# A fused attention and mixture-of-experts kernel: the order of the last two heads, of the last batch's routing, and of the first expert's rows

## The reference

```python
# first block: attention with squared scores and a decay
qk = einsum('bthd,bshd->bhts', q, k) * scale
a = where(causal, qk**2 * exp(logG[t] - logG[s]), 0)
y = einsum('bhts,bshd->bthd', a, v) / (sum(a, -1) + 1e-6)
x1 = layernorm(x + y.reshape(B, T, 2048) @ Wc + bc)
# second block: 6 of 64 experts for each token, and a shared one
scores = softmax(x1 @ gate_w.T); w, idx = top_k(scores, 6); w /= sum(w)
# rows of x1 go to (expert, place in it); places beyond the capacity are dropped
eo = (silu(buf @ w_gate[e].T) * (buf @ w_up[e].T)) @ w_down[e].T
y = sum of w * eo over a token's experts + (silu(x1 @ sg.T) * (x1 @ su.T)) @ sd.T
out = layernorm(x1 + y)
```

## Time and profile before

| | |
|---|---|
| median of 3 runs | 2256.55 us (2251.35 to 2260.19) |
| profiled execution | 2263.97 us |
| its span | 2262.2 us, mean granted clock of PE 0.979 |
| busy: PE, PEld | 2145.9 us (95%), 1960.7 us (87%) |
| busy: DVE, ACT, POOL | 1293.0 (57%), 1162.2 (51%), 751.1 us (33%) |

### The profile page before, as it was taken

The page is one execution under the profiler, slowest core; times in us unless marked ns, Lnnn a source line. Parts: engine busy times, 40 slices in busy tenths (PEclk is TensorE's granted clock), DMA queues, the critical chain, the costliest instruction groups (busy, mean ns, idle before and its releaser), DMA issues.

```text
span 2262.2 us, 38643 instructions
## 1 busy us (share of the span) xinstructions
PE 2145.9 (95%) x14567; PEld 1960.7 (87%) x14570; DVE 1293.0 (57%) x2851; ACT 1162.2 (51%) x2201; POOL 751.1 (33%) x751
## 2 busy tenths in 40 slices
PE   8999999999999999999999999999886899999993
PEld 6999998999889899889989898999765789999992
DVE  4444444444666345455644556545663688888876
ACT  4444544444444445444444444445433577777875
POOL 3121112100004520000352001440242478878885
PEclk9999999999999999999999999999997999999996
DMA  4866732112112311211241211321343789999977
GB/s 168 334 275 263 294 107 71 46 61 73 36 59 97 134 53 54 80 36 56 82 140 58 80 61 51 102 83 63 107 150 133 184 198 237 235 221 238 234 154 239
DMA packets 146642, 302.28 MB, mean 134 GB/s; under 512 B 20336, under 2 KB 82544, under 8 KB 146448
## 3 DMA queue, kind: packets, MB, share of 16 engines
q1 hardware_dynamic: 104960, 247.34, 32.2%
q0 software_dynamic: 41056, 51.96, 11.6%
q10 hardware_dynamic: 432, 0.44, 0.1%
HBM read 160.57 MB, written 142.67 MB: 134 GB/s over the span
## 4 chain that ended last, share of the span: by engine, by line
PE 79%; DVE 8%; issue 4%; ACT 3%; POOL 3%; DMA 2%; another core or an unknown queue 1%; POOLq 0%; ACTq 0%; SPq 0%; DVEq 0%
PE bank L951 48%; PE bank L1360 21%; PE bank L960 5%; PE bank L1373 2%; POOL y_part L2421 2%; PE bank L1478 1%; DMA y_part<-y_e,row_token 1%; DVE ub L1966 1%; DVE xe_lo L2243 1%; DVE stats L2326 0%; DVE bank L2150 0%; ACT q_hi L1638 0%; ACT silu_b L1712 0%; POOL slots L2411 0%
## 5 line engine op out<-in xcount | busy, mean ns | idle before, releaser
L1360 PEld LDWEIGHTS bank<-v,a 128*128 128x128 f32 x4608 | 605.5, 191 | 44.2 <-ACT a L1662 0.5
L1360 PE MATMUL bank<-v,a 128*128 128x129 f32 x4608 | 618.6, 275 | 0.3 <-ACT a L1662 0.3
L2421 POOL DMA_INDIRECT y_part<-y_e,row_token x234 | 359.1, 1535 | 147.9 <-ACT y_e L1779 77.1
L2394 POOL TENSOR_TENSOR decay_all<-decay_all,tab 128x128 f32<-128x128 f32 x128 | 60.2, 471 | 918.3 <-DMA decay_all<-decay_dram 917.9
L1658 ACT ACTIVATE a<-bank,c_s 128x512 f32<-128x512 f32 x384 | 263.1, 686 | 184.2 <-PE bank L951 170.8
L1662 ACT ACTIVATE a<-ub 128x512 f32<-128x512 f32 (+1 forms) x256 | 133.8, 523 | 376.9 <-DVE ub L1966 355.3
L2411 POOL DMA_INDIRECT slots<-rows,slot_u x192 | 189.2, 985 | 319.6 <-PE bank L1360 140.8
L951 PE MATMUL bank<-q_hi,k_hi 128*128 128x512 f32 (+1 forms) x640 | 262.9, 411 | 7.5 <-DVE ub L1966 7.5
L1945 DVE TENSOR_TENSOR q_lo<-bank,q_hi 128x512 fp32r<-128x512 f32 x128 | 88.5, 692 | 273.2 <-ACT q_hi L1638 269.8
L951 PE MATMUL bank<-q_lo,k_hi 128*128 128x512 f32 (+1 forms) x640 | 238.5, 373 | 0.0
L951 PE MATMUL bank<-q_hi,k_lo 128*128 128x512 f32 (+1 forms) x640 | 237.3, 371 | 0.0
(11 more groups left out here) (247 smaller groups left out, 4761.8 us busy)
## 6 DMA issues: line engine op xcount, KB each, us to landing
slots<-acc SPq DMA_DIRECT2D x64, 816.0 KB, 7.8
w_raw_f<-in_wffn SPq DMA_DIRECT2D x68, 624.0 KB
decay_all<-decay_dram SPq DMA_DIRECT2D x128, 128.0 KB
xr<-slots SPq DMA_DIRECT2D x18, 544.0 KB
xr<-slots SPq DMA_DIRECT2D x20, 476.0 KB
w_hi<-w_dram SPq DMA_DIRECT2D x24, 384.0 KB
w_lo<-w_dram SPq DMA_DIRECT2D x24, 384.0 KB
wc_hi<-wc_dram SPq DMA_DIRECT2D x24, 256.0 KB
```

The source lines that it names most:

```text
L1360: ins = e.matmul(dst[:, tt, r, :], a32[u % NA][:, r, t0:t0 + P], v[n % 3][:, s, :], start=(s == 0 and r == 0), stop=(s == 2 * g + tt), ski ...
L2394: e.tensor_tensor(arg[:, GROUP:GROUP + P], arg[:, P:GROUP], mask, ALU.add)
L2421: e.indirect_dma_start(out=y_part[part], out_offset=bass.IndirectOffsetOnAxis(ap=token, axis=0), in_=y_rows, in_offset=None, bounds_check= ...
```

## The change

The last two heads take turns by groups of queries: group 2 of each, then group 3 of each, with the places of `em`, `decay_all` and the loads of the decay taken by the group's number in the order (`em_at`). The last batch is routed in three parts, a half and two quarters. The steps of the first half, and those of the first quarter up to `softmax0`, are tied to units by a table, `route_at`; `TOGETHER` is gone. Both sends of the first half are now in the attention. A part of one pair has no `again`. The shared jobs are no longer split around the routing in the same places, and the first expert's rows are turned ahead of the last `shared_end`. The buffers of the experts' rows are taken by `x_at(place)`; with M1 = 6 blocks this is the parity of the place, as before. Two of ACT's copies of shared results no longer wait for the store of x1t.

```diff
-LAST_UNITS = (diagonal(LAST, 0) + before(LAST, 1) + before(LAST + 1, 1)[:1] + diagonal(LAST, 1) + before(LAST + 1, 1)[1:]
-              + diagonal(LAST + 1, 0) + diagonal(LAST + 1, 1) + before(LAST, 2) + before(LAST, 3) + diagonal(LAST, 2)
-              + diagonal(LAST, 3) + before(LAST + 1, 2) + before(LAST + 1, 3) + diagonal(LAST + 1, 2) + diagonal(LAST + 1, 3))
+HEAD_A, HEAD_B = LAST, LAST + 1
+LAST_UNITS = (diagonal(HEAD_A, 0) + before(HEAD_A, 1) + before(HEAD_B, 1)[:1] + diagonal(HEAD_A, 1) + before(HEAD_B, 1)[1:]
+              + diagonal(HEAD_B, 0) + diagonal(HEAD_B, 1) + before(HEAD_A, 2) + before(HEAD_B, 2)[:2] + diagonal(HEAD_A, 2)
+              + before(HEAD_B, 2)[2:] + before(HEAD_A, 3)[:2] + diagonal(HEAD_B, 2) + before(HEAD_A, 3)[2:] + before(HEAD_B, 3)
+              + diagonal(HEAD_A, 3) + diagonal(HEAD_B, 3))
...
-PARTS = [(b_, 0, TILES) for b_ in range(B - 1)] + [(B - 1, t_, TILES // 2) for t_ in (0, TILES // 2)]
+PARTS = ([(b_, 0, TILES) for b_ in range(B - 1)] + [(B - 1, 0, TILES // 2)]
+         + [(B - 1, t_, TILES // 4) for t_ in (TILES // 2, TILES * 3 // 4)])
+FIRST_HALF, QUARTER_A, QUARTER_B = B - 1, B, B + 1
...
-             + [f"{what}{q}" for q in pairs for what in ("again", "send")])
+             + [f"{what}{q}" for q in pairs for what in ("again", "send") if what == "send" or len(pairs) > 1])
...
-TOGETHER = ("stat0", "norm0", "norm1", "store", "softmax1", "chosen_bf", "weight0")
...
-        "em": {(L, 0): -5, (L, 1): -3, (L + 1, 0): 0, (L + 1, 1): 4, (L, 2): 12, (L, 3): 17, (L + 1, 2): 26, (L + 1, 3): 31},
-        "em_mask": {(L, 0): -7, (L, 1): -4, (L + 1, 0): -1, (L + 1, 1): 1, (L, 2): 10, (L, 3): 15, (L + 1, 2): 24, (L + 1, 3): 29},
-        "decay_in": {(L, 0): -11, (L, 1): -7, (L + 1, 0): -4, (L + 1, 1): -2, (L, 2): 1, (L, 3): 5, (L + 1, 2): 13, (L + 1, 3): 18}}
+        "em": {(L, 0): -5, (L, 1): -3, (L + 1, 0): 0, (L + 1, 1): 4, (L, 2): 12, (L + 1, 2): 17, (L, 3): 26, (L + 1, 3): 31},
+        "em_mask": {(L, 0): -7, (L, 1): -4, (L + 1, 0): -1, (L + 1, 1): 1, (L, 2): 10, (L + 1, 2): 15, (L, 3): 24, (L + 1, 3): 29},
+        "decay_in": {(L, 0): -11, (L, 1): -7, (L + 1, 0): -4, (L + 1, 1): -2, (L, 2): 1, (L + 1, 2): 5, (L, 3): 13, (L + 1, 3): 18}}
     cols_at = {-3: (1, 0, 0), -2: (0, 0, 0), -1: (0, 1, 0), 4: (1, 0, 1), 7: (0, 0, 1), 10: (0, 1, 1)}
-    first_half_routed_at = 19
+    route_at = {17: [(FIRST_HALF, "stat0")], 18: [(FIRST_HALF, "stat1"), (FIRST_HALF, "std")],
+                20: [(FIRST_HALF, step) for step in ("norm0", "norm1", "store")], 22: [(FIRST_HALF, "x1t0")],
+                23: [(FIRST_HALF, "logit0")], 24: [(FIRST_HALF, "x1t1")], 25: [(FIRST_HALF, "logit1")],
+                26: [(FIRST_HALF, "softmax0")], 27: [(FIRST_HALF, "softmax1"), (FIRST_HALF, "max")], 28: [(FIRST_HALF, "index")],
+                29: [(FIRST_HALF, "hot0"), (FIRST_HALF, "chosen0")],
+                30: [(FIRST_HALF, step) for step in ("hot1", "chosen1", "chosen_bf")],
+                31: [(FIRST_HALF, step) for step in ("weight0", "weight1", "count")] + [(QUARTER_A, "stat0")],
+                32: [(FIRST_HALF, "slots"), (QUARTER_A, "std")], 33: [(FIRST_HALF, "again0"), (FIRST_HALF, "send0")],
+                34: [(FIRST_HALF, "again1"), (FIRST_HALF, "send1")], 35: [(QUARTER_A, "norm0"), (QUARTER_A, "store")],
+                37: [(QUARTER_A, "x1t0")], 38: [(QUARTER_A, "logit0")], 39: [(QUARTER_A, "softmax0")]}
...
-        elif background and u >= step_from and background[0] != (B - 1, "again1"):
+        elif background and u >= step_from:
             p, name = background.pop(0)
             route_step(p, name)
-            while p == B - 1 and name in TOGETHER:
-                p, name = background.pop(0)
-                route_step(p, name)
-
             step_from = u + (2 if p < B - 2 else 1)
...
+    def turn(x_id):
+        for pair in range(pairs_of(x_id)):
+            on_spare("turn_x", x_id, pair)
+        do("pick", x_id)
+
+    def split(x_id):
+        do("split_hi", x_id)
+        for part in range(3):
+            do("split_lo", x_id, part)
+
     catch_up()
     do("shared_in", 2)
     up(0, 0)
     do("experts_begin")
     send_all()
+    on_spare("project", L, NG - 1)
+    on_spare("turn", L + 1, NG - 1)
     up(0, 1)
-    on_spare("turn", HEADS - 1, NG - 1)
-    do("turn_lo", HEADS - 1, NG - 1)
+    do("add", L, NG - 1)
+    do("turn_lo", L + 1, NG - 1)
+    route(QUARTER_A, "softmax1", "max", "index")
+    on_spare("project", L + 1, NG - 1)
     up(0, 2)
     gated(0, 0)
-    on_spare("project", HEADS - 1, NG - 2)
+    do("add", L + 1, NG - 1)
+    route(QUARTER_B, "stat0", "std")
     gated(0, 1)
-    up(1, 0)
-    do("add", HEADS - 1, NG - 2)
-    on_spare("project", HEADS - 1, NG - 1)
-    route_to("stat0")
+    route(QUARTER_A, "hot0", "chosen0", "chosen_bf")
+    up(1)
+    route(QUARTER_A, "weight0", "weight1", "count")
     gated(0, 2, 3)
-    up(1, 1)
-    do("add", HEADS - 1, NG - 1)
     do("shared_in", 3)
-    route_to("std")
-    up(1, 2)
+    route(QUARTER_B, "norm0", "store")
     gated(1, 0)
-    route_to("store")
+    up(2, 0)
+    route(QUARTER_A, "slots", "send0")
     gated(1, 1)
-    up(2, 0)
-    route_to("x1t0")
-    on_spare("route", *second[1])
-    x1t1 = second.pop(1)
+    route(QUARTER_B, "x1t0")
+    up(2, 1)
     gated(1, 2, 3)
-    up(2, 1)
-    route_to("logit0")
+    route(QUARTER_B, "logit0")
     up(2, 2)
-    route_to("logit1")
-    route_to("softmax0")
+    route(QUARTER_B, "softmax0")
     shared_end(0)
-    for step in background:
-        route_step(*step)
-        send_all()
     gated(2, 0)
-    route_to("max")
+    route(QUARTER_B, "softmax1", "max")
     gated(2, 1, 2, 3)
     up(3)
-    route_to("index")
-    route_to("chosen0")
+    route(QUARTER_B, "index", "hot0", "chosen0", "chosen_bf")
     gated(3, 0)
     up(4)
-    gated(3, 1, 2, 3)
-    route_to("chosen1")
+    gated(3, 1)
+    route(QUARTER_B, "weight0", "weight1", "count")
+    gated(3, 2, 3)
     shared_end(1)
-    route_to("weight1")
+    route(QUARTER_B, "slots", "send0")
+    assert not any(to_route.values())
+    do("rank_keys")
     gated(4, 0)
-    up(5, 0)
-    gated(4, 1, 2, 3)
-    route_to("count")
-    up(5, 1, 2)
-    route_to("slots")
-    route_to("send0")
-    up(6)
-    gated(5)
-    shared_end(2)
-    route_to("send1")
-    assert not second
-    do("rank_keys")
+    up(5)
     on_spare("rank_experts")
     for x_id in MAINS[:4]:
         do("raw_in", x_id)
-    up(7)
-    gated(6)
-    for m in range(3, M1 - 2):
-        up(2 * m + 2)
-        gated(2 * m + 1)
-        shared_end(m)
-        up(2 * m + 3)
-        gated(2 * m + 2)
-    up(2 * M1 - 2)
-    gated(2 * M1 - 3)
-    do("split_hi", MAINS[0])
-    for part in range(3):
-        do("split_lo", MAINS[0], part)
-    up(2 * M1 - 1)
-    gated(2 * M1 - 2)
-    do("rows_in", MAINS[0])
-    do("rows_in", MAINS[1])
-    do("extra_in", E)
-    shared_end(M1 - 2)
-    gated(2 * M1 - 1)
+    gated(4, 1, 2, 3)
+    for k in range(6, KX):
+        up(k)
+        gated(k - 1)
+        if k == max(6, KX - 3):
+            split(MAINS[0])
+        if k == KX - 2:
+            do("rows_in", MAINS[0])
+            do("rows_in", MAINS[1])
+            do("extra_in", E)
+        if k % 2 == 0:
+            shared_end(k // 2 - 1)
+    gated(KX - 1)
     do("rows_in", MAINS[2])
-    do("split_hi", MAINS[1])
-    for part in range(3):
-        do("split_lo", MAINS[1], part)
+    turn(SEQ[0])
+    split(MAINS[1])
     shared_end(M1 - 1)
     for i in range(1, EXTRA):
         do("extra_in", E + i)
     do("counted",)
 
-    def turn(x_id):
-        for pair in range(pairs_of(x_id)):
-            on_spare("turn_x", x_id, pair)
-        do("pick", x_id)
-
     def down(x_id, pairs):
         for pair in pairs:
             if pair < pairs_of(x_id):
                 on_spare("down", x_id, pair)
 
-    turn(SEQ[0])
...
+        def x_at(place):
+            return (M1 + place) % 2
...
             def turn_x(x_id, pair_):
                 m = spare["turn_x", x_id, pair_]
                 once.wait_ge(s_spare, m + 1)
-                once.wait_ge(c_gu, 3 * (KX + max(PLACE[x_id] - 1, 0)))
-                turned_hi(bank[6 + m % 2], PLACE[x_id] % 2, tiles_in_pair(x_id, pair_), shape_of(x_id)[1])
+                once.wait_ge(c_gu, 3 * (KX + PLACE[x_id] - 1) if PLACE[x_id] else 3 * 2 * (M1 - 1))
+                turned_hi(bank[6 + m % 2], x_at(PLACE[x_id]), tiles_in_pair(x_id, pair_), shape_of(x_id)[1])
...
-                if m_ >= 2:
-                    once.wait_ge(s_x1t_out, 16 * 2 * NG * B)
```

More of the change, by code:

```diff
@@ L397, in schedule @@
             background = route_steps(n // H - 1)
-        if u - u_last == first_half_routed_at:
+        for step in route_at.get(u - u_last, ()):
             assert not background
-            background = route_steps(B - 1)
+            route_step(*step)
         if (n + 2) % H == 0 and n + 2 < HEADS:
@@ L409, in schedule @@
                 do("x_rest", b1, x_split_at.index(at))
```

(42 more changed lines are left out.)

12 lines of the change are left out of this document (6 added, 6 removed).

## The result

The changed kernel takes 2264.89 us (median of 20 runs, 2255.71 to 2273.71), the kernel before 2260.17 us (20 runs, 2251.35 to 2264.01): ratio 1.0022, 95% interval 1.0014 to 1.0031. The forecast was 2233 us. The profiled execution of the changed kernel took 2267.0 us, span 2265.3.

What follows compares the result with a forecast made beforehand. PE's order was the bound, with only its idle time and slow clock to win. -8.2 + 7.1 - 27 + 1 = -27 us gave 2237 on the profiled execution, 2229.5 off the median; 2233 us was taken between, range 2219 to 2256.

Steps and rivals of the forecast that it cites:

- 2.3 at the count: Attention's end: PE waits 2.3 us at the first half's count, because chosen_bf ends late on DVE.
- 1.4 at the mask: Attention's end: the mask of unit 37 stands behind the first send, a PE wait of 1.4 us.
- 3.7 at x1t0: Attention's end: the quarter's x1t0 stands behind both sends, the mask, a decay and the norm, 3.7 us.
- The turn of the first expert's rows: Moved ahead of shared_end(5): waits of 4.15 and 1.4 us go, one of 2.4 comes, winning 3.2 us.
- the first half's `rows`: At 1586 us: earlier routing removes PE's 3.2 us wait and 5.0 of slow clock, -8.2 us; clock there 1.00.
- why the crawl should go: PE's slow stretch, 1690 to 1716 us, beside 24 scatters goes by splitting them: 18.2 us and about 2 of clock.
- Rival (1): The crawl moves to the new scatter bursts, giving back 20 us: 2253, no change; chance 0.15.
- Rival (2): The crawl is the profiler's, absent from timed runs; the change is then -7: 2249; chance 0.12.
- the slow clock: Wins 5.0 us behind the `rows` wait; in the shared jobs 9 us of slow clock become 5.
- the far bound: Attention's end: +12 us in place of +7.1, all of DVE's 9 us excess with a slow clock of 3.
- the saving in the shared jobs: 1622 to 1760 us: waits fall from 35.3 to 12.5 us, slow clock from 9 to 5: -27 us.
- -7 of the rest: The whole change's worth without 20 us of crawl: -7 us.

Runs made afterwards that it cites:

- after_nosend: The changed kernel without the last batch's 48 scatters: 2252.0 us, the kernel before beside it 2259.6.
- after_paced: The changed kernel with the last batch's scatters paced by units and by PE's up products: 2257.0 us, the kernel before beside it 2259.6.
- units_nosend: The kernel before without its last 48 scatters, the last two heads taking turns by groups of queries: 2232.8 us, the kernel before beside it 2238.1.
- burst24: The kernel before with only the last 24 of the last batch's scatters, in one row: 2257.8 us, the kernel before beside it 2260.6.
- before_two: The kernel before with all its scatters, at most two of the last batch's under way: 2249.2 us, the kernel before beside it 2259.5.
- after_two_late: The changed kernel, last 48 scatters behind the clearing of `hb`, at most two under way: 2252.4 us, the kernel before beside it 2238.1.
- after_again: The changed kernel once more, unaltered, on a chip of the second kind: 2253.3 us, the kernel before beside it 2237.6.
- before_nosend: The kernel before without the last batch's 48 scatters: 2231.3 us, the kernel before beside it 2259.6.

## Why the prediction was wrong

**What held.** The size of the waits. For PE at the attention's end I had 2.3 at the count, 1.4 at the mask, 3.7 at x1t0; after_nosend has 2.89, 0.51 and 3.51, and 0.9 twice at the first half's logits, which I had not. In the shared jobs I had 12.5 us in all, and 14.9 are there: 2.4 at up(2) (2.3 forecast), 1.4 for `x1t_lo` (2.3), 1.5 at up(4) (1.0), 2.9 at shared_end(1) (3.1), 2.8 at shared_end(5) (2.4), and one of 3.3 at up(6) that I had missed. The turn of the first expert's rows did what I had: 2.8 in place of 5.6. No PE wait for the first half's `rows` is left, but the clock there is 0.94 and not 1.00.

**First failed step: "why the crawl should go".** I took nothing for the new bursts because bursts of 12 showed no "remote" wait before. Without scatters the changed kernel gains 13 us, so that much crawl stayed in it. The evidence that I gave for a harmless burst of 12 was wrong even in the trace of before: two updates of PE were late beside those bursts (2.0 us at 1634, 0.8 at 1671), too short to show as a "remote" wait. The lead was no safe measure either: late updates stand beside leads of 12.1 us in the changed kernel and of 6.2 in after_paced. Rival (1) named this course, with 20 us given back and 2253 as its time; it was the crawl's course, not the kernel's. Rival (2), a crawl of the profiled execution alone, is refuted: removing the scatters takes 28 us off the median of all runs. But each of these runs has its span and clock on record, so a part of the recording in the crawl is not excluded (see "Open").

**Second failed step: the slow clock.** I gave the clock -5.0 behind the first wait and -4 in the shared jobs, a gain of about 9. That size was one execution's. The same wait of some 3.2 us stands in 13 traces with the old routing: two (before, units_nosend) have 10.2 us at half clock beside it, two (burst24, before_two) 3.4, and nine none. The changed order has slow clock in all five of its traces: at the wait of 3.5 us at unit 37 stand 17.1 us at half clock (after), 10.2 (after_nosend), 6.8 (after_two_late), 6.8 (after_again) and 3.4 (after_paced). From 1606 to 1622 us PE is busy 10.5 to 12.3 us in them, and 15.5 in the earlier trace rows. On the way to the first expert the clock fell 7 times in after_nosend, which has six waits of 2.4 to 3.5 us there, and once in before_nosend, which has four of 2.0 to 4.2; so the waits' length alone does not tell it. I had most of these waits, priced each at its length, and added 5 us of slow clock in the shared jobs and none at the attention's end, where 3 us stood only in the far bound. Measured, it is 17.0 us in all.

**Third: the saving in the shared jobs.** Before has 13.7 us of waits there once the scatters are out of the way, not the 17.1 that I took as ordinary (35.3 - 18.2): the wait for the clearing of `hb`, which stood behind six scatters, was also theirs. So 13.7 became 14.9, where I had 17.1 become 12.5. Most of the 2.4 us beyond the forecast are the 3.3 at up(6) that I had missed.

The sum: I had -20 of crawl and -7 of the rest, from a base of 2256.55 us that 20 runs put at 2260.17. On the chips of the first kind the crawl went from 28 to 13, -15, and the rest is +20.7, where I had -7; together 5 to 6, and 4.7 in the first result. That they add up is no test of them, since both terms are differences of the same times. On the second kind the changed kernel has no late update, and the whole is +15.7.

**Open.** Which part brings the slow clock is not shown by a run of its own. By their medians the order of units and the earlier first half cost nothing alone; the turn ahead was not run in the change's place. What is left, the two quarters and both sends at the attention's end, together with the rest, is argued and not shown.

Why PE's updates are late beside a long queue of scatters, and only on some chips, is open too: the runs show that it takes the scatters, that a wait on their landing removes it, and that the products stand in the record as done. One difference between the chips points at a rival that no run tests. On the chips of the second kind the traces hold every update of PE's semaphores. In every trace of the first kind, and in the two of the first result, some 4 to 5% of them are missing, and about a seventh of all updates, those of DMAs among them: of the same program, the trace of the first result holds 20,312 and that of after_again 23,846. They are missing in before_nosend as well, which has no crawl. So the recording itself may be what holds up PE on these chips; an execution without it is not on record.

## What to carry to other kernels

An engine that "waits for remote" while its producer stands done in the trace is not waiting for work: compare the semaphore's update with the end of the instruction that makes it, and take out the suspected traffic once, to price it, before building an order around it. Where long rows of GpSimd's indirect DMAs cost time, try a wait on the landing of an earlier one, on semaphores used in turns: two under way took every late update away on the first kind of chip, and three kept the start each 1.28 us on the second. Keep what others wait for, such as a memset, ahead of DMAs that now wait. And don't take a slow clock from one execution, nor price new waits at their length alone: after_nosend lost 17 us of speed over a stretch with six waits of 2.4 to 3.5 us, before_nosend 3.4 over one with four of 2.0 to 4.2.

## What was not expected of the hardware

PE's semaphore updates came at least 10.5 us, and counted product by product up to 22.5 us, behind the end of the products while 24 indirect DMAs stood in GpSimd's queue, and then five within 0.3 us; DVE's and ACT's were never late. The Trainium skill's page "Advanced Engine Details and Errata", section Engine Queue Depths, gives GpSimd 8 places. The traces do not agree, if a place is one scatter: in the earlier trace rows the sequencer had passed the last one 15.6 us, or 12 scatters, before it started. On the chips of the first kind each long row of the last batch had late updates beside it, and no kernel that kept to two under way had one there. On a chip of the second kind the sequencer ran 11 scatters ahead without one, so a long queue is not enough. The same program, before, took 2260 us on two chips and 2238 on two others.
